# Two more of every four right-hand heads transposed by DMA in the middle samples of an attention kernel

## What is computed

```python
q, k, v = x @ Wq.T, x @ Wk.T, x @ Wv.T          # 32 query heads, 8 key and value heads of 128
q, k = rope(rmsnorm(q)), rope(rmsnorm(k))
k_all = concat([k_cache[block_table], k])       # 512 + 128 keys a sample
v_all = concat([v_cache[block_table], v])
scores = q @ k_all.T / sqrt(128); scores[keys >= cache_seqlens] = -1e30
o = softmax(scores) @ v_all
x = x + o @ Wo.T
```

## Time and the profile before

| | |
|---|---|
| median of three runs | 1293.41 us |
| lowest, highest | 1292.99, 1294.8 us |
| the profiled execution's own time | 1293.98 us |
| its span, first to last instruction | 1292.4 us |
| mean granted clock of TensorE in it | 1.000 |
| one unit in the loop (first score of a unit to the next unit's) | 31.09 us |

### The profile page before, as it was taken

The page is one execution under the profiler, slowest core; times in us unless marked ns, Lnnn a source line. Parts: engine busy times, 40 slices in busy tenths (PEclk is TensorE's granted clock), DMA queues, the critical chain, the costliest instruction groups (busy, mean ns, idle before and its releaser), DMA issues.

```text
span 1292.4 us, 25910 instructions
## 1 busy us (share of the span) xinstructions
PE 1277.1 (99%) x6713; PEld 1091.7 (84%) x6713; DVE 936.2 (72%) x2658; ACT 785.5 (61%) x1834; POOL 766.1 (59%) x792
## 2 busy tenths in 40 slices
PE   9999999998999999999999999999999999999998
PEld 8888877887888888888888888888888878888886
DVE  6532457778777777877777788777777887777774
ACT  6731333556666668576666676766667767666664
POOL 3110011348766668688666686966667869666663
PEclk9999999999999999999999999999999999999999
DMA  8321224286555557766555677555556765655543
GB/s 293 106 82 49 74 71 142 55 269 202 127 124 122 126 134 214 186 132 128 131 129 128 142 203 188 127 137 133 133 131 179 186 164 128 131 131 124 124 91 82
DMA packets 314893, 179.55 MB, mean 139 GB/s; under 512 B 260418, under 2 KB 279234, under 8 KB 314562
## 3 DMA queue, kind: packets, MB, share of 16 engines
q1 hardware_dynamic: 295840, 125.83, 40.6%
q0 software_dynamic: 12032, 35.40, 10.1%
q10 hardware_dynamic: 6946, 17.44, 4.2%
HBM read 119.71 MB, written 16.91 MB: 106 GB/s over the span
## 4 chain that ended last, share of the span: by engine, by line
PE 93%; DVE 4%; issue 1%; ACT 1%; DMA 0%; POOL 0%; ACTq 0%; POOLq 0%; DVEq 0%
PE bank L1625 20%; PE wide L1695 16%; PE tail L1663 15%; PE tail L1732 14%; PE wide L464 4%; PE wide L1657 4%; PE bank L1646 3%; PE wide L544 3%; PE bank L464 3%; PE tail L464 3%; PE wide L599 2%; PE bank L544 1%; PE bank L599 1%; PE tail L530 1%; DVE prT L2090 1%
## 5 line engine op out<-in xcount | busy, mean ns | idle before, releaser
L1663 PE MATMUL tail<-prT,vt 128*128 128x512 f32 (+1 forms) x975 | 257.1, 403 | 0.2
L1663 PEld LDWEIGHTS tail<-prT,vt 128*128 128x128 f32 x975 | 171.9, 189 | 39.0 <-DVE prT L2090 10.1
L1343 POOL TENSOR_TENSOR tick<-tick 128x1 f32<-128x1 f32 x254 | 57.3, 225 | 212.4 <-PE tail L1663 71.1
L1732 PE MATMUL tail<-woT,oT 128*128 128x512 f32 x768 | 179.5, 389 | 0.9 <-DVE oT L2142 0.9
L1732 PEld LDWEIGHTS tail<-woT,oT 128*128 128x128 f32 x768 | 144.1, 188 | 31.2 <-DVE oT L2142 1.3
L1695 PE MATMUL wide<-kT,qT 128*128 128x320 f32 x512 | 159.7, 312 | 6.3 <-DVE mx L2118 2.5
L1695 PE MATMUL wide<-kT_low,qT 128*128 128x320 f32 x512 | 158.1, 309 | 0.0
L1695 PE MATMUL wide<-kT,qT_low 128*128 128x320 f32 x512 | 157.9, 308 | 0.0
L1401 POOL TENSOR_TENSOR parts<-raw,parts 128x1280 f16<-128x1280 f32 x55 | 145.6, 2647 | 8.0
L1885 ACT ACTIVATE raw<-raw,nm,q_scale 128x640 f32<-128x640 f32 x124 | 114.6, 924 | 43.6 <-DVE nm L2121 42.1
L1885 ACT ACTIVATE pr<-pr,nm,q_scale 128x640 f32<-128x640 f32 x128 | 117.9, 921 | 33.9 <-DVE nm L2121 32.9
(11 more groups left out here) (289 smaller groups left out, 2905.8 us busy)
## 6 DMA issues: line engine op xcount, KB each, us to landing
w_ring<-pair_weights SPq DMA_DIRECT2D x80, 256.0 KB, 4.1
k_raw<-k_pages SPq DMA_DIRECT2D x512, 32.0 KB, 1.7
v_raw<-v_pages SPq DMA_DIRECT2D x512, 32.0 KB, 3.2
spread<-one_over_denominators ACTq DMA_DIRECT2D x32, 512.0 KB, 4.9
xTb<-x_transposed POOLq DMA_DIRECT2D x31, 512.0 KB, 4.3
rope<-rope_tables SPq DMA_DIRECT2D x31, 256.0 KB, 2.7
out<-y POOLq DMA_DIRECT2D x31, 256.0 KB, 5.4
w_raw<-w_gate_up SPq DMA_DIRECT2D x10, 512.0 KB, 3.2
```

The lines of the kernel that those rows point to most:

```text
L1343: nc.gpsimd.tensor_tensor(tick[:, 2:3], tick[:, 1:2], tick[:, 1:2], ALU.add).then_inc(s_carry, 1)
L1663: last = nc.tensor.matmul(tail[g][:, first * S:end * S], vt[v_part][:, j, g * D:(g + 1) * D], prT[p_part][:, first:end, j, :], start=(j == ...
L1732: last = nc.tensor.matmul(place[:, :], oT[:, g, o_part, (h % REP) * S:(h % REP + 1) * S], woT[w_part][:, h, :], start=(h == o_part == w_pa ...
```

## The change

`THIRDS = range(2, 6)`: for samples 2 to 5 of each of the four pairs, 16 of the 32 units, heads 4 and 5 take the DMA way too, as a third pair of heads. Their two `pr` tiles are now one tensor `pr_third`.

- GpSimd halves them after heads 2 and 3 (`halve_third`) into the same `parts[0]` that heads 0 and 1 left, and widens the low part in the next turn, after `split_keys` (`low_turned_third`). `add_share` comes behind that, and `share_room` between the two `halve`.
- SyncE issues 14 pages of keys, the first transpose, 2 pages of keys, the other three transposes, seven of the sixteen value pages, two more transposes (`turn_third`) and nine value pages.
- ScalarE widens the high part (`high_turned_third`) over `prT[0]` of heads 0 and 1, once TensorE has summed those; `spread_shares` moves from ahead of the two query and key casts to behind them, with `spread` at another address.
- TensorE transposes ten instead of twenty tiles, in another order; the sums of g = 1 do all high parts first and then all low parts.
- In every turn the load of `xTb` goes from GpSimd's queue to ScalarE's.
- The loops hold three units instead of five (two are written out for each pair).
- In the four turns with a late root, its steps go between the first four `mask_max`, its values lie in `bank[1]`, and TensorE waits for it ahead of the first product that overwrites `bank[1]`, not ahead of `score(1)`.

```diff
+    THIRDS = range(2, 6)
...
+        def halve_third(u, before, n):
+            pool.wait_ge(s_exp, u * HP + 3 * HALF)
+            for i in range(2):
+                pool.wait_ge(s_turned[0][i], (u + before) * 16 + 16)
+            carry(n)
+            nc.gpsimd.tensor_copy(parts[0][:, 0], pr_third[:, :, :]).then_inc(s_half, 1)
+            pool.wait_ge(s_half, u * 2 + before + 3)
+            nc.gpsimd.tensor_tensor(parts[0][:, 1], pr_third[:, :, :], parts[0][:, 0], ALU.subtract).then_inc(s_rest[0], HALF)
+        def low_turned_third(u, before, n):
+            pool.wait_ge(s_turned[0][1], (u + before) * 16 + 32)
+            pool.wait_ge(s_pv, u * G + 1 + FIRST)
+            carry(n)
+            nc.gpsimd.tensor_copy(prT[1][:, 0:HALF].rearrange("p h j q -> p (h j) q"), turned_third[1]).then_inc(s_tl, 1)
...
+        def turn_third(pair, b):
+            u, before = unit(pair, b), thirds(pair, b)
+            sp.wait_ge(s_rest[0], (u + before) * HALF + 2 * HALF)
+            for i in range(2):
+                sp.sem_inc(s_seen, 1)
+                sp.dma_start_transpose(turned_third[i], parts[0][:, i].rearrange("p h n -> p (h n)")).then_inc(s_turned[0][i], 16)
...
+            def high_turned_third():
+                act.wait_ge(s_turned[0][0], (u + before_back) * 16 + 32)
+                ac.copy(prT[0][:, 0:HALF].rearrange("p h j q -> p (h j) q"), turned_third[0]).then_inc(s_th[0], 1)
...
             def spread_shares():
-                act.wait_ge(s_turned[0][1], u * 16 + 16)
+                act.wait_ge(s_turned[1][1], u * 16 + 16)
...
+            if third:
+                pe.wait_ge(s_yadd, u + FIRST)
+                pe.wait_ge(s_th[0], u + before_back + 2)
+                for w in range(2):
+                    pe.wait_ge(s_phi, u * 3 + w + 1)
+                    sums(1, (2 * w, 2 * w + 1), (0, 1), 0)
+                pe.wait_ge(s_phi, u * 3 + 3)
+                sums(1, (JT - 1,), (0, 1), 0)
+                for w in range(2):
+                    pe.wait_ge(t_free[w], u + 1 + FIRST)
+                pe.wait_ge(s_tl, u * 2 + before_back + 3)
+                sums(1, range(JT - 1), (0,), 1)
+                begin(0)
+                sums(1, (JT - 1,), (0,), 1).then_inc(s_pv, 1)
```

More of the change, by code:

```diff
@@ L1432, in turn @@
                 n = n + 1
+            if has_third(b - 1):
+                low_turned_third(u - 1, thirds(pair, b - 1), n)
+                add_share(u - 2, share, n + 1)
+                n = n + 2
             if left:
@@ L1462, in turn @@
                 split_values(u, n, not extra)
-                halve(u, n + 1, 0, False, extra != "next")
-                halve(u, n + 2, 1, False, then_x is not None and extra != "next")
+                halve(u, before, n + 1, 0, False, extra != "next")
+                if has_third(b - 1):
+                    share_room(u, True)
+                halve(u, before, n + 2, 1, False, then_x is not None and extra != "next")
+                if has_third(b):
+                    halve_third(u, before, n + 3)
+                    n = n + 1
                 if extra == "next":
@@ L1520, in load_rope, with load_values @@
                          rope_scratch[bass.ds(b, 1)].rearrange("o p n -> (o p) n")).then_inc(s_ropel, 16)
-        def load_values(pair, b, pages):
+        def load_values(pair, b, pages, first=0, end=NPP):
             sp.wait_ge(s_vs, unit(pair, b) + FIRST)
-            for j, page in enumerate(pages):
+            for j in range(first, end):
+                page = pages[j]
                 i = j % (P // PSIZE)
@@ L1609, in begin @@
                 pe.wait_ge(c_free[i], full[i].value() + FIRST)
+            before_back, third = thirds(pair, b - 1), back and has_third(b - 1)
             first_turn = isinstance(b, int) and b == 0
@@ L1638, in project_ahead @@
                     which, step = divmod(first, NPROD)
+                    if which and step == 0 and second_queries_late(pair, b, front, back):
+                        pe.wait_ge(s_second_root, second_queries_late(pair, b, front, back) * ROOT_STEPS)
                     count = min(end - first, NPROD - step)
@@ L1777, in turn @@
                     rest.fourth_quarter()
-                pe.wait_ge(s_rope, n * G + 2 + FIRST)
-                transposes(0, [ra[:, REP + i, :] for i in range(G)])
-            if back and front:
+                if not third:
+                    pe.wait_ge(s_rope, n * G + 2 + FIRST)
+                    transposes(0, [ra[:, REP + i, :] for i in range(G)])
+            if back and front and not third:
                 sums(0, (2, 3), (0,), 1, low_heads)
@@ L1829, in turn @@
             full0 = Count(c_full[0], before[0])
+            before_front, before_back, third = thirds(pair, b), thirds(pair, b - 1), back and has_third(b - 1)
+            first_head = HALF if third else 0
+            heads_there = REP - first_head
             def arrive():
@@ L1953, in turn @@
                 arrive()
-                squares(0, REP + G, REP, s_q1)
+                squares(0, REP + G, REP)
                 if not back:
                     act.wait_ge(s_xs[0], 16 * BLK)
+                if ahead and not third:
+                    load_x((b + 1) % B if isinstance(b, int) else b + 1)
+                if not back:
                     for i in range(3 * KT, 4 * KT + 1):
@@ L1961, in turn @@
                 if share or not front:
-                    high_turned(u, 1, False)
+                    high_turned(u, before_back, 1, False)
+                if third and ahead:
+                    load_x(b + 1)
             early(0)
@@ L1965, in turn @@
                 copy_share()
-            if back:
+            if back and not third:
                 spread_shares()
@@ L2029, in turn @@
             n, u = unit(pair, b), unit(pair, b - 1)
+            before_front, third = thirds(pair, b), back and has_third(b - 1)
+            first_head = HALF if third else 0
+            heads_there = REP - first_head
             full1 = Count(c_full[1], before[1])
@@ L2067, in inverse_root, with first_root_of @@
                 done(v.tensor_scalar(q_scale[:, 1, heads], y, -SCALE, None, ALU.mult))
+            def first_root_of(heads):
+                for _ in inverse_root(heads, (x_[:, heads], root[:, heads]), then):
+                    pass
+            second = slice(REP + G, NH)
+            second_root = inverse_root(second, [bank[1][:, i * REP:(i + 1) * REP] for i in range(2)], then_second)
             def rotate(h0, m0, kinds):
@@ L2204, in turn @@
                         normalise(1)
-                    if back and h == 1:
+                    if late and h < 4:
+                        if h == 0:
+                            dve.wait_ge(c_free[1], before[1] + 3 + FIRST)
+                        next(second_root, None)
+                    if back and h == (5 if late else 1):
                         low_values(0)
-                    if back and h == 3:
+                    if back and h == (6 if late else 3):
                         low_values(1)
```

261 lines of the change are left out of this document (153 added, 108 removed).

## The result

| | before | changed |
|---|---|---|
| median | 1293.41 us | 1277.38 us |
| lowest to highest | 1292.99 to 1294.8 | 1275.63 to 1278.3 |
| profiled execution, its span | 1293.98, 1292.4 | 1275.63, 1273.9 |

The account below looks back on a forecast made before the run. TensorE, without idle time in a 31.09 us unit, was the bound. 16 x (1.15 - 0.1) = 16.8 us, less 0.5 for first turns, gave 16.3; 1293.98 - 16.3 = 1277.7, median 0.6 lower: 1277.1 us, range 1271.5 to 1285.

Parts of the forecast that it names:

- Ten transposes, 1.15 us a unit: TensorE's queue: ten transposes fewer per unit with a third pair, priced by distances between starts at 1.15 us gross.
- A new wait for ScalarE, 0.1 us: TensorE waiting for ScalarE's first probability cast, ready at 720.2 to 720.6 against 720.3: 0 to 0.3 us, taken as 0.1.
- the term of the loop: Gain of the sixteen units with a third pair: 16 x (1.15 - 0.1) = 16.8 us.
- First turns, 0.5 us: First turns, where ScalarE has one issue more: a loss of 0.5 us in total.
- The late roots, 0: Four late-root turns: root steps between VectorE's maxima, TensorE waiting before overwriting bank[1]; -1.4 to +1 us each, taken as 0.
- GpSimd, +5 us a unit: GpSimd's added casts, subtraction and carries: +5 us, about 26 of a unit of 30, not the bound.
- The third transposes, landing after 3.4, at most 5.9 us: SyncE's two new transposes, issued at 712.6 and 714.0, were to land 3.4 us later, at most 5.9, and stay hidden.
- Spread load (rival 3): Spread load, issued 3 us later behind more traffic, lands late; VectorE then TensorE stall; slower, up to 1320 us; chance 0.05.
- GpSimd's halving at 707.6 on the old clock: GpSimd starts halving heads 4 and 5 at 707.6, ends 711.8; low parts end 714.6, 1.1 us before ScalarE's query cast.
- From the spans to the median: The profiled execution was forecast at 1277.7 us, and the median 0.6 us lower, at 1277.1.
- The signs: First-score distances 29.9 to 30.1 us with a third pair, 31.09 without; wrong if the former stay 31 or unchanged units move over 0.1.
- The chance of 0.88 for faster: Probability that the whole kernel gets faster, against 0.05 for the same time (1290.8 to 1296 us) and 0.07 for slower.

Follow-up runs that it names:

- the split of the keys: Changed kernel, SyncE issuing 11 key pages, two transposes, then 5 pages in units with a third pair, not 14, one transpose, 2, one: 1288.71 us.

## Why the prediction was right

1277.1 us was forecast, 1277.38 measured. The mechanism is the one named: ten transposes leave a queue that is never idle, and the chains in their place are in time. That the number fits to 0.3 us is luck: several terms were off, and cancel.

- **Ten transposes, 1.15 us a unit.** Measured 1.16 in the unit shown. The kernel without the third pair confirms the size from the other side: 17.7 us over 16 units, 1.1 each (waits and order included). The sums gave another 0.24 us that I had not priced, and the `ra` transposes took 0.17 back.
- **A new wait for ScalarE, 0.1 us.** None in the profile: 0, with a cover of under 0.2. So 1.20 us a unit came, not 1.05; the term of the loop was 2.4 us too small.
- **First turns, 0.5 us.** 1.04 in the first unit in this profile, 0.2 to 1.2 over the ten kernels with `xTb` loaded ahead of the stores of one over the denominators, 0.1 or less with it moved. The term of 0.5 was of the right size.
- **The late roots, 0.** The three turns of the later pairs moved by +0.67, -0.12 and -0.89, in one profile; the +0.67 goes with the spread landing of 9.6 us. With the old root the time is the same within its interval.
- **GpSimd, +5 us a unit.** 25.11 instead of 20.64 us busy, so +4.5. Its third low part had its cover as forecast in most units, and next to none in one.
- **The third transposes, landing after 3.4, at most 5.9 us.** Measured 3.4 to 7.1, median 3.8. They were issued 5.9 us behind the projection, as forecast, in the first unit of three runs, and 6.1 to 8.2 behind it in the others.
- **Spread load (rival 3).** In the loop it is hidden, as forecast. Its median landing fell to 4.2 us, below the 5 to 6.5 forecast, but at two of the three changes of pair it took 9.6 and 9.3, and VectorE waited 1.6 us for it once, more than the 1 us that I had given as a sign. I had put a landing of that size at 5% and for the loop. It came outside the loop, through a move that I had priced at nothing (the load "is needed after the next score(0), over ten us later: nothing"): I had asked who waits for that load, not what waits behind it in the DMA engines.
- **GpSimd's halving at 707.6 on the old clock.** The step that was wrong. It holds in the first unit of each run (0.7 to 0.8 us behind the projection), but not in the next three: 1.4 to 3.9 us behind it. I had looked at three more key pages and seen a SyncE that waited there; but its whole queue had grown. The rope table, with which a unit's issues begin, goes out 12.8 us ahead of the projection in the unit shown, where it was 16.4, so the first transpose leaves 4.6 us ahead of it instead of 6.1. The three rows of before, with the projection at 706.71, and those of the changed kernel, with it at 700.04, are below. The cover of 1.1 us for ScalarE's query cast was used up (1.85 us of waiting). That cost nothing, for a reason the prediction did not have: the key cast behind it waits for TensorE until then.

```profile
690.30 0.36 SPq L1519 DMA_DIRECT2D rope<-rope_tables  x1
690.91 5.61 SPq L1513 DMA_DIRECT2D k_raw<-k_pages  x11
700.61 8.20 SPq L1552 DMA_TRANSPOSE turned<-parts  x4
```

```profile
687.20 0.36 SPq L1559 DMA_DIRECT2D rope<-rope_tables  x1
687.82 7.34 SPq L1553 DMA_DIRECT2D k_raw<-k_pages  x14
695.47 1.39 SPq L1594 DMA_TRANSPOSE turned<-parts  x1
```

- **From the spans to the median.** The terms above give 18.5 us in the profiled executions, 16.0 in the medians. The three other executions of the changed kernel took 1276.7 to 1278.3, that is 1.1 to 2.7 us more within their spans. That moving one load narrows this to 1 us and takes 3.4 us off the median points to the changes of pair and the first unit, where kernels that differ in one edit elsewhere vary by up to 1 us a turn; the longer executions themselves were not profiled, so this stays open.
- **The signs.** Distances were 29.83 to 30.05 us with a third pair and 31.08 to 31.10 in the like turns without one, as given. The first unit and the turns with a late root did not stay within 0.1 us, as the terms above say.
- **The chance of 0.88 for faster** rested on covers of 0 to 0.8 us. They held, but one value page ahead instead of seven ate all of the gain, and the split of the keys two thirds.

## What to carry to other kernels

When one engine is busy all the time, price a change by the distances between starts on that engine, and then list for each other chain the moment at which it is due; the gain is whole only while no cover is used up; here the smallest were 0 and under 0.2 us. Count the issuing queue as a chain too, over the whole loop: an issue that waits in the middle holds back all behind it, and putting other issues into that hole (seven pages, not one or fifteen) was worth more here than an early start. Of a transfer that is moved ask also what it now runs ahead of: a load that nobody needs soon can delay one that somebody does.

## What was not expected

- With the keys split, the new transposes went out later, by 1.4 us in the unit shown; where one of them also took 5.8 to 6.7 us to land, the unit became 2 to 4.5 us longer. An issue order that is better for one buffer was worse for the kernel.
- A load of 512 KB ahead of another in ScalarE's queue made the second one land 7.5 to 10.9 us after its issue in nearly all profiles, instead of 5.3 to 7.2. Up to 9.2 us it cost nothing.
- The kernel without the third pair, with the rest of the change, had executions from 1293.8 to 1299.0 us, while the kernel before stayed within 0.7 us beside it. Its programs are longer, since two units of each pair are written out; whether that matters was not tried.
